# Prologue of a four-layer kernel: low parts of five units on VectorE, distance table first, first pair's rows requested at the fourth unit, maxima stored by ScalarE's queue

## The chip, the cores and the metric

The kernel runs on one core of one Trainium2 chip. The metric is the device time in microseconds (us) of one execution, given as the median of several; lower is better. Engines are named as the profile names them: PE (TensorE matmul), PEld (its weight loads), DVE (VectorE), ACT (ScalarE), POOL (GpSimd), SP (SyncE, which here only issues DMAs). "SPq" is SP's own instruction stream; "DMA queue" is what it hands transfers to.

## The reference, cut to what matters

Four post-norm layers follow one another: softmax attention with a distance decay, an FP4-quantised gated FFN, linear attention, and a mixture of experts. The change touches only what stands ahead of the first one.

```python
q = (x @ Wq.T + bq).reshape(B, T, H, hd)        # B=2, T=2048, D=256, H=16, hd=16
k = (x @ Wk.T + bk).reshape(B, T, H, hd)
v = (x @ Wv.T + bv).reshape(B, T, H, hd)
scores = jnp.einsum('bqhd,bkhd->bhqk', q, k) * scale
scores = scores * jnp.exp(-alpha * lag)          # lag = |i - j|
attn = softmax(scores); out = attn @ v
```

## The kernel before

The kernel is a row of stages, each a block in which the five engines run their own instruction streams; a stage begins when every engine has left the one before. The first stage, `stage_prologue`, makes q, k and v; the second, `stage_attention`, goes through 16 pairs of heads (`Pair`).

**Units.** The prologue works through `GROUPS` = 16 units. Unit u is batch u // 8, half `jt` of the 256 columns of q and k (u // 4 % 2), and a chunk of 512 positions (u % 4). For a unit PE computes a q tile and a k tile (`project`, four matmuls; it is called for unit u + 1 in steps 4 and 5 of unit u), ACT copies them to `full` (L531, L534), and POOL makes one or two versions of q scaled by the table `grow` (L597). So a unit has three or four variants: KEY, LEFT and/or RIGHT, RAW. Each variant is split into three bf16 parts that add up to the f32 value: ACT writes the high part (L545), DVE subtracts it (`split`, L610), ACT writes the middle part (`middle`, L512), and POOL subtracts that and writes the low part (`low`, L559). POOL does `low(u - 1)` in the pass for unit u. `full` has three buffers (`FULLS`), so ACT's evacuation of unit u waits for the low parts of unit u - 3.

**Stores and loads.** When a unit's low parts are done, SP stores its parts to DRAM with four DMAs of 384 KB (L415, into `scr`); units with `jt` = 1 also have v, which SP stores with one DMA of 1 MB (L422, into `vscr`). Units 0 to 3 hold every position of the first eight heads, so they hold all rows of the first pair, `Pair(0, 0)`. SP requests those rows with `load_p1`: 12 DMAs (L312) into `p1`, for q and for k, for two heads each, in three runs of 3, 2 and 1 times 16 rows of 4 KB (`RUNS`). This is written after the stores of unit 4 (`if u == QB`). `load_p2` (18 DMAs) and the second pair's `load_p1` come behind units 7 and 9.

**Tiles.** With the first pair's rows PE and DVE find the largest score of each row ahead of the attention: 128 tiles, each one matmul of 512 columns (L474) and one multiply-and-max on DVE with the distance table `toep` (L626), through two PSUM banks (`PBANKS`). They are spread evenly over the steps of the units from `WITH_TILES` on (`tiles_behind`). After unit 15 come 26 tiles of the second pair and one transposition of the maxima (`SKEWED`), after which `turn_maxima` writes `mt` and `mparts`; SP stores these and loads them again (`store_maxima` and `load_maxima`, 4 and 8 DMAs).

**Small pieces.** POOL clears two borders of `part` (L574, L575), makes `toep` in its pass for unit 1 (L581), and clears 24 rows of `p2[0]` in its pass for unit 3 (L589). A table of decay factors goes from DVE (`cev`, L658, written at the start of DVE's pass for unit 2) to DRAM and back into `p2[0]` by SP (L402, six DMAs, and L405, two); SP does this ahead of all stores of units.

DVE stores a v tile into one of two buffers and, from the third unit with v on, first waits until the DMA of the v before last has landed (`vout`).

Of the kernel before, what the change touches and what calls it, by code (L numbers as in the profile page):

```python
# [6 lines left out]
ALU = mybir.AluOpType  # L7
# [37 lines left out]
    "p_": "loaded dist expd ident cdist cexp csplit ctr cev prep wload xload0 xload1 qk_ps v_ps vout qk_ev "  # L45
          "v_ev scaled hi rest mid low out0 out1 vset",
    "a_": "setup waug p1load0 p1load1 p2load0 p2load1 vload0 vload1 mload0 mload1 mbc ring_full ring_free "
# [48 lines left out]
def up_to(n):  # L96

    return n + 1
# [168 lines left out]
FULLS = 3  # L267
WITH_TILES = 5
STEPS = 8
# [89 lines left out]
def stage_prologue(nc, g, a, p1, p2, vp, mx):  # L359

    with ExitStack() as ctx:
# [24 lines left out]
        def chunk_of(u):  # L386

            b, jt, chunk = place(u)
            return b * QB + chunk if jt else None

        with nc.Block() as block:
            @block.sync
            def _(sp):
# [5 lines left out]
                sp.dma_start(bv[:], a["bv"].partition_broadcast(P)).then_inc(s["wload"], 16)  # L399
                sp.wait_ge(s["cev"], up_to(1))  # L400
                for r, e in enumerate(K_PARTS):
                    sp.dma_start(g["w6"][r].rearrange("q (t p) -> (q t) p", p=P), wt[:, e, :]).then_inc(s["loaded"], 16)  # L402
                sp.wait_ge(s["loaded"], up_to(48 + 16 * 6))
                for hh in range(2):
                    sp.dma_start(p2[0][ROWS:ROWS + AUG, hh, KEY, :],  # L405
                                 g["w6"].rearrange("r q t -> (r q) t")).then_inc(sa["waug"], 16)
# [100 lines left out]
            def _(act):  # L507
# [11 lines left out]
                for u in range(GROUPS):  # L519
# [7 lines left out]
                    if u >= FULLS:  # L527

                        act.wait_ge(s["low"], up_to(parts_upto(u - FULLS + 1)))
                    act.wait_ge(s["qk_ps"], up_to(2 * u + 1))  # L530
# [11 lines left out]
                    for i, var in enumerate(parts_of(u)):  # L542
                        if var in (LEFT, RIGHT):
                            act.wait_ge(s["scaled"], up_to(scaled_upto(u) + i))
                        act.activation(part[:, chunk, var, 0, :], full[:, u % FULLS, var, :], ACT.Copy).then_inc(s["hi"], 1)  # L545
                middle(GROUPS - 1)

            @block.gpsimd
            def _(pool):
# [6 lines left out]
                def low(u):  # L556
                    for i, var in enumerate(parts_of(u)):
# [15 lines left out]
                                   base=0, pattern=[[-1, P]], channel_multiplier=1).then_inc(s["ident"], 1)  # L573
                pool.memset(part[:, 0, LEFT, :, :], 0.0).then_inc(s["ident"], 1)  # L574
                pool.memset(part[:, QB - 1, RIGHT, :, :], 0.0).then_inc(s["ident"], 1)  # L575
                pool.sem_inc(sa["exp"], EXP0)
                pool.sem_inc(sa["value"], PV0)
                pool.sem_inc(sa["evac"], EV0)
                for u in range(GROUPS):
                    if u == 1:  # L580
                        pool.iota(toep[:], [[-1, TOEP]], base=OFF, channel_multiplier=1,  # L581
                                  allow_small_or_imprecise_dtypes=True).then_inc(s["dist"], 1)
                    if u == 0:
                        load_x(2)
                        load_x(3)
                    if u == 3:
                        pool.wait_ge(s["scaled"], up_to(scaled_upto(u)))
                        pool.wait_ge(s["low"], up_to(parts_upto(u - 1)))
                        pool.memset(p2[0][ROWS:ROWS + AUG, :, LEFT:RIGHT + 1, :], 0.0).then_inc(sa["setup"], 1)  # L589
                        pool.wait_ge(sa["setup"], up_to(1))  # L590
                    if QB < u <= 2 * QB:
# [12 lines left out]
            def _(dve):  # L604
# [16 lines left out]
                def tile(slot, j, n):  # L621
# [6 lines left out]
                                             mp[:, j, hh * TB + qt, kc:kc + 1]).then_inc(sa["ring_free"], 1)  # L628

                dve.wait_ge(s["loaded"], up_to(48))  # L630
                dve.tensor_scalar(nalpha[:], alpha[:], -1.0, None, ALU.mult).then_inc(s["prep"], 1)
# [23 lines left out]
                for u in range(GROUPS):  # L655
                    if u == 2:
                        dve.wait_ge(s["ctr"], up_to(1))
                        dve.tensor_copy(wt[:], ps_t).then_inc(s["cev"], 1)  # L658
                        dve.memset(vsb[:], 0.0).then_inc(s["vset"], 1)
                        dve.wait_ge(s["vset"], up_to(1))  # L660
                        dve.memset(vsb[:, :, :, :, :, HD:HD + 1], 1.0).then_inc(s["vset"], 1)
                        dve.wait_ge(s["vset"], up_to(2))
# [11 lines left out]
                for i, n in enumerate(SKEWED):  # L674
# [4 lines left out]
                    else:  # L679
                        tile(slot, 1, n)  # L680
                dve.wait_ge(s["ident"], up_to(4))

# [1902 lines left out]
```

## Time and profile before

| what | value |
|---|---|
| median of 3 runs | 3417.16 us (3413.48, 3422.5, 3417.16) |
| the profiled execution, its own time | 3417.1 us |
| its span, first to last instruction | 3415.3 us |
| mean granted TensorE clock | 0.95 |
| first instruction of the attention stage | 282.49 us into the span |

The prologue is thus 8% of the span. A timeline row reads: start, length, engine, line, operation, written tile <- read tile, count, and in brackets how long the engine had been idle before it and what ended that.

### The profile page before, as it was taken

What the parts mean: (1) busy time and instruction counts of PE and PEld (TensorE: products, weight loads), DVE (VectorE), ACT (ScalarE), POOL (GpSimd) and SP (SyncE); (2) the same over time, 40 slices, a digit from 0 to 9 for tenths busy, and PEclk for the clock granted to TensorE, in tenths of its full rate; (3) what the DMA queues carried; (4) which work ended last, traced back from release to release, by engine and by line L of the source; (5) the groups of instructions that cost most, each with busy time, mean ns of one, the idle gap of its engine ahead of it and who ended that gap; (6) DMA issues with size and microseconds to landing.
All of it is one profiled execution on the core that took longest, in us unless ns stands there. A gap on an engine that the chain in (4) does not pass through costs nothing. (4 is left out here: it accounts for less than half of the span.)

```text
span 3415.3 us, 66017 instructions
## 1 busy us (share of the span) xinstructions
PE 3071.1 (90%) x22948; PEld 1734.7 (51%) x22949; DVE 2440.1 (71%) x6509; ACT 1802.2 (53%) x2255; POOL 1422.7 (42%) x741
## 2 busy tenths in 40 slices
PE   3678999999999999999985998989999987999996
PEld 1232333333333333333323565556666666999995
DVE  4679999999999999999747888844555554333334
ACT  4235888888888888888873333322222222111112
POOL 6346787878878787787801000000000111111110
PEclk7788999999999999999997999989899988999998
DMA  5575434332344443333204110030000005555555
GB/s 154 144 192 138 90 84 83 79 78 76 67 91 92 93 89 82 83 79 78 57 13 78 25 38 5 1 99 14 14 14 14 23 18 191 183 182 177 182 184 182
DMA packets 201698, 304.65 MB, mean 89 GB/s; under 512 B 86192, under 2 KB 150544, under 8 KB 199248
## 3 DMA queue, kind: packets, MB, share of 16 engines
q1 hardware_dynamic: 192640, 277.89, 31.6%
q0 software_dynamic: 7632, 22.16, 1.8%
q8 instruction: 159, 2.61, 0.3%
q14 instruction: 115, 0.94, 0.1%
q10 hardware_dynamic: 1152, 1.05, 0.1%
HBM read 238.91 MB, written 62.13 MB: 88 GB/s over the span
## 5 line engine op out<-in xcount | busy, mean ns | idle before, releaser
L870 DVE CUSTOM_DVE_ANT_0 ps_r<-ps_r,toep 128x512 f32<-128x512 f32 x1894 | 1252.3, 716 | 71.8 <-PE ps_r L799 31.6
L969 ACT ACTIVATE prob<-ps_s,csc 128x1024 f32<-128x1024 f32 x768 | 829.9, 1118 | 151.4 <-PE ps_s L823 129.6
L927 POOL TENSOR_TENSOR tb<-tb,toep 128x1024 f32<-128x1024 f32 x240 | 568.1, 2367 | 264.0 <-ACT tb L959 229.4
L799 PE MATMUL ps_r<-p 96*128 96x512 bf16 x1894 | 646.3, 382 | 10.1 <-DVE mp L870 4.1
L823 PE MATMUL ps_s<-p 120*128 120x512 bf16 (+1 forms) x2048 | 609.3, 380 | 27.1 <-ACT tb L959 16.4
L930 POOL TENSOR_TENSOR tb<-tb,mb 128x1024 f32<-128x1024 f32 x240 | 567.8, 2366 | 18.8
L839 PE MATMUL ps_o<-prob,vp 128*32 128x256 f32 x8192 | 548.2, 385 | 1.2 <-ACT prob L966 0.9
L799 PEld LDWEIGHTS ps_r<-p 96*128 96x128 bf16 x1894 | 181.4, 96 | 406.2 <-DVE mp L870 258.0
L1695 POOL DMA_INDIRECT slots_scratch<-l_xh,l_place x64 | 62.5, 976 | 710.3 <-DVE l_xh L2020 693.3
L839 PEld LDWEIGHTS ps_o<-prob,vp 128*32 128x32 f32 x8192 | 213.7, 109 | 269.6 <-issue 177.9
L823 PEld LDWEIGHTS ps_s<-p 120*128 120x128 bf16 (+1 forms) x2048 | 189.6, 98 | 237.2 <-ACT tb L959 46.6
L2335 ACT ACTIVATE e_aT<-e_u 128x1024 f32<-128x1024 f32 x71 | 75.0, 1057 | 421.4 <-DVE e_u L2406 421.4
L966 ACT ACTIVATE prob<-tb 128x1024 f32<-128x1024 f32 x256 | 272.3, 1064 | 2.9 <-POOL tb L930 2.8
L2281 PEld LDWEIGHTS ps_eu<-e_hT,moe_w 128*128 128x128 f32 x2272 | 266.3, 193 | 7.7 <-DVE e_hT L2397 4.1
L2281 PE MATMUL ps_eu<-e_hT,moe_w 128*128 128x128 f32 x2272 | 266.9, 276 | 3.5 <-DVE e_hT L2397 3.5
L870 DVE DVE_READ_ACCUMULATOR2_ANT mp<- 128x1 f32 x1894 | 266.2, 141 | 0.0
L959 ACT ACTIVATE tb<-ps_s 128x1024 f32<-128x1024 f32 x240 | 247.0, 1029 | 32.7 <-PE ps_s L823 31.3
L2374 POOL DMA_INDIRECT ytok_scratch<-e_y,e_name x71 | 69.2, 975 | 463.0 <-DVE e_y L2452 463.0
L2299 PE MATMUL ps_ed<-moe_w,e_aT 128*128 x1136 | 257.0, 379 | 0.8 <-DVE e_y L2452 0.8
L2406 DVE TENSOR_TENSOR e_u<-ps_eu,moe_cols 128x1024 f32<-128x1024 f32 x71 | 86.9, 1224 | 210.1 <-PE ps_eu L2281 210.1
L2299 PEld LDWEIGHTS ps_ed<-moe_w,e_aT 128*128 128x128 f32 x1136 | 210.3, 190 | 26.9 <-issue 1.2
L1280 PE MATMUL ps_du<-wgu,d_xs 128*128 128x512 f32 (+1 forms) x384 | 164.6, 580 | 4.2 <-DVE d_h L1559 2.6
(324 smaller groups left out, 3580.4 us busy)
## 6 DMA issues: line engine op xcount, KB each, us to landing
moe_w<-in_W_dram SPq DMA_DIRECT2D x79, 1024.0 KB, 5.3
p<-scr_scratch SPq DMA_DIRECT2D x288, 192.0 KB
mb<-mrow_scratch SPq DMA_DIRECT2D x16, 2048.0 KB, 7.4
scr_scratch<-part SPq DMA_DIRECT2D x64, 384.0 KB, 6.7
p<-scr_scratch SPq DMA_DIRECT2D x96, 128.0 KB
moe_pt<-slots_scratch SPq DMA_DIRECT2D x72, 132.0 KB, 2.1
vscr_scratch<-vsb SPq DMA_DIRECT2D x8, 1024.0 KB, 8.8
vp<-vscr_scratch SPq DMA_DIRECT2D x16, 512.0 KB, 22.2
```

Source lines behind the costliest of these rows:

```text
L799: pe.matmul(ps_r[:, bank, :], buf[:, hh, 0, qt * P:(qt + 1) * P], buf[:, hh, 1, kc * CH:(kc + 1) * CH], start=True, stop=True)\
L823: mm = pe.matmul(ps_s[:, n % 2, hh, :], buf[0:rows, hh, KEY, kb * P:(kb + 1) * P], buf[0:rows, hh, var, qb * CH:(qb + 1) * CH], start=True ...
L839: mm = pe.matmul(out.rearrange("p (j c) -> p j c", c=P), vp[whose.par][:, kb, hh, :], prob[:, m % RING, hh, :].rearrange("p (j f c) -> p f ...
L870: dve.tensor_tensor_reduce(ps_r[:, bank, :], ps_r[:, bank, :], toep[:, col:col + CH], 1.0, -3.0e38, ALU.mult, ALU.max, mp[:, whose.par, hh ...
L927: pool.tensor_tensor(tb[:, k % DIAGS], tb[:, k % DIAGS], toep[:, col:col + CH].unsqueeze(1) .broadcast_to([P, 2, CH]), ALU.mult).then_inc( ...
L930: pool.tensor_tensor(tb[:, k % DIAGS], tb[:, k % DIAGS], mb[:, this.par, :, qb * CH:(qb + 1) * CH], ALU.add).then_inc(s["less"], 1)
L959: act.activation(tb[:, k % DIAGS], ps_s[:, (mine - 1) % 2], ACT.Copy).then_inc(s["copied"], 1)
L966: act.activation(prob[:, n % RING], tb[:, k % DIAGS], ACT.Exp).then_inc(s["exp"], 1)
L969: act.activation(prob[:, n % RING], ps_s[:, mine % 2], ACT.Exp, scale=csc[:, qb * TB + kb:qb * TB + kb + 1]).then_inc(s["exp"], 1)
L1280: mm = pe.matmul(ps_u[:, lo:hi], xs[:, c % 2, kc, t * P:(t + 1) * P], wgu[:, kc, lo:hi], start=(kc == 0), stop=(kc == KC - 1), skip_group_ ...
L2281: mm = pe.matmul(ps_u[:, tile.par, f, :], w1[:, tile.par, kc, f * P:(f + 1) * P], hT[:, kc, :], start=(kc == 0), stop=(kc == KC - 1), skip ...
L2299: mm = pe.matmul(ps_d[:, 0:D], aT[:, this.par, f, :], w["w2"][:, bass.ds(e, 1), f, :].rearrange("p a n -> p (a n)"), start=(f == 0), stop= ...
```

## The change

Five things are done at once in `stage_prologue`; no arithmetic of the result changes.

1. The low parts of units 0 to 4 (`LOW_FIRST` = 5) are made on DVE, in a function `low` of its own that counts on a semaphore `lowv`; POOL makes those of units 5 to 15. Whoever waits for low parts asks `low_done`.
2. `toep` is made by POOL before its loop over units. The two borders of `part` and the 24 rows of `p2[0]` are cleared by DVE.
3. SP stores units 0 and 1 first, then sends the decay table out and back, then goes on with unit 2. It requests the first pair's rows right behind unit 3, once the stores of units 0 to 3 have landed.
4. `WITH_TILES` is 6: PE waits for the first pair's rows at unit 6, not at unit 5, and the 128 tiles are spread over ten units.
5. The maxima are stored and loaded by ACT's queue, after ACT's last middle part.

```diff
-WITH_TILES = 5
+WITH_TILES = 6
+LOW_FIRST = 5
...
+        def low_done(eng, u):
+            if u < LOW_FIRST:
+                eng.wait_ge(s["lowv"], up_to(parts_upto(u + 1)))
+            else:
+                eng.wait_ge(s["low"], up_to(parts_upto(u + 1) - parts_upto(LOW_FIRST)))
...
             def _(sp):
...
-                sp.wait_ge(s["cev"], up_to(1))
-                for r, e in enumerate(K_PARTS):
-                    sp.dma_start(g["w6"][r].rearrange("q (t p) -> (q t) p", p=P), wt[:, e, :]).then_inc(s["loaded"], 16)
...
                 for u in range(GROUPS):
-                    sp.wait_ge(s["low"], up_to(parts_upto(u + 1)))
+                    low_done(sp, u)
...
+                    if u == 1:
+                        sp.wait_ge(s["cev"], up_to(1))
+                        for r, e in enumerate(K_PARTS):
+                            sp.dma_start(g["w6"][r].rearrange("q (t p) -> (q t) p", p=P), wt[:, e, :]).then_inc(s["loaded"], 16)
...
-                    if u == QB:
-                        sp.wait_ge(s["out1"], up_to(64 * 2))
+                    if u == QB - 1:
+                        for n in range(2):
+                            sp.wait_ge(s[f"out{n}"], up_to(64 * 2))
                         load_p1(sp, Pair(0, 0))
...
-                sp.wait_ge(sa["setup"], up_to(1))
-                sp.wait_ge(sa["ring_free"], up_to(TILES + TURN + 1))
-                store_maxima(sp, g, sa, mt, mparts)
-                sp.wait_ge(sa["mstore"], up_to(64))
-                load_maxima(sp, g, sa, p2[0], "mload0")
...
             def _(act):
...
+                act.wait_ge(sa["setup"], up_to(1))
+                act.wait_ge(sa["ring_free"], up_to(TILES + TURN + 1))
+                store_maxima(act, g, sa, mt, mparts)
+                act.wait_ge(sa["mstore"], up_to(64))
+                load_maxima(act, g, sa, p2[0], "mload0")
...
             def _(pool):
...
-                    if u:
+                    if u > LOW_FIRST:
                         low(u - 1)
...
             def _(dve):
...
+                    if u == 3:
+                        dve.memset(p2[0][ROWS:ROWS + AUG, :, LEFT:RIGHT + 1, :], 0.0).then_inc(sa["setup"], 1)
...
+                    if 1 <= u <= LOW_FIRST:
+                        low(u - 1)
```

**SP, from the first store on.** In the kernel before, the order of DMA issues on SP is this (`w_scratch` and `p_0<-w_scratch` are the decay table, `scr_scratch<-part` the stores of units, four each, `p_0<-scr_scratch` the first pair's rows):

```order
L402 DMA w_scratch<-wt 64x128 x6
L405 DMA p_0<-w_scratch 24x2048 x2
L415 DMA scr_scratch<-part 32x12x512 x20
L422 DMA vscr_scratch<-vsb 128x8x256
L312 DMA p_0<-scr_scratch 48x1x2048 x2
L312 DMA p_0<-scr_scratch 32x1x2048 x2
```

In the changed kernel (its lines are numbered anew):

```order
L415 DMA scr_scratch<-part 32x12x512 x8
L427 DMA w_scratch<-wt 64x128 x6
L430 DMA p_0<-w_scratch 24x2048 x2
L415 DMA scr_scratch<-part 32x12x512 x8
L313 DMA p_0<-scr_scratch 48x1x2048 x2
L313 DMA p_0<-scr_scratch 32x1x2048 x2
```

Two units' stores moved ahead of the table, and one unit's stores and one store of v moved behind the request.

**DVE, its passes for units 0 to 4.** Before, DVE has only its subtractions and the start of the v buffer there:

```order
L610 TENSOR_TENSOR full<-full,part 128x512 x7
L658 COPY wt<-ps_pr 64x384
L659 MEMSET vsb 128x4096
L661 MEMSET vsb 128x128
L610 TENSOR_TENSOR full<-full,part 128x512 x10
```

In the changed kernel the low parts (L634) stand between them, and the clearing of `p_0`'s rows (L673), which is written there as 2 x 2048 elements:

```order
L611 TENSOR_TENSOR full<-full,part 128x512 x3
L634 TENSOR_TENSOR part<-full,part 128x512 x3
L611 TENSOR_TENSOR full<-full,part 128x512 x4
L667 COPY wt<-ps_pr 64x384
L668 MEMSET vsb 128x4096
L670 MEMSET vsb 128x128
L634 TENSOR_TENSOR part<-full,part 128x512 x4
L611 TENSOR_TENSOR full<-full,part 128x512 x4
L673 MEMSET p_0 24x2x2048
L634 TENSOR_TENSOR part<-full,part 128x512 x4
L611 TENSOR_TENSOR full<-full,part 128x512 x3
L634 TENSOR_TENSOR part<-full,part 128x512 x3
```

**POOL, the same stretch.** Before, POOL's order there, its low parts being L559 and the clearing of the same rows L589 (written as 2 x 4096 elements):

```order
L559 TENSOR_TENSOR part<-full,part 128x512 x3
L597 TENSOR_TENSOR full<-full,grow 128x512 x2
L559 TENSOR_TENSOR part<-full,part 128x512 x4
L589 MEMSET p_0 24x2x4096
L597 TENSOR_TENSOR full<-full,grow 128x512
L559 TENSOR_TENSOR part<-full,part 128x512 x4
```

In the changed kernel seven scalings (L598) follow one another with nothing between them:

```order
L583 IOTA toep 128x3968
L562 DMA xc<-in_xT_dram 128x2x512 x2
L598 TENSOR_TENSOR full<-full,grow 128x512 x7
L562 DMA xc<-in_xT_dram 128x2x512
```

What left POOL here is the seventeen low parts of units 0 to 4 and the clearing; the table `toep` moved ahead of its first scaling.

## Rows read from the trace of the kernel before

**Rows 1.** The page, its head.

```profile
span 3415.3 us, 66017 instructions
```

**Rows 2.** Waits of 0 to 282 us: who for whom, total, times, longest.

```profile
PE ps_v L464 <- DMA p<-scr_scratch: 58.3, 1, 58.3
...
DVE vsb L618 <- DMA vscr_scratch<-vsb: 7.0, 1, 7.0
```

**Rows 3.** Timeline of PE around the first pair's rows.

```profile
42.73 3.70 PE L454 MATMUL ps_qk<-xc,w_qkv 128*128 128x512 f32 x8 [1.64 <-ACT full L534]
104.74 2.04 PE L464 MATMUL ps_v<-w_qkv,xc 128*128 128x256 f32 x4 [58.30 <-DMA p<-scr_scratch]
...
111.50 1.88 PE L454 MATMUL ps_qk<-xc,w_qkv 128*128 128x512 f32 x4
...
124.52 1.88 PE L454 MATMUL ps_qk<-xc,w_qkv 128*128 128x512 f32 x4
```

**Rows 4.** Timeline of SP's issues, from several windows of 30 to 105 us.

```profile
33.02 3.72 SPq L402 DMA_DIRECT2D w_scratch<-wt  x6
...
38.85 11.87 SPq L415 DMA_DIRECT2D scr_scratch<-part  x8
...
65.69 3.27 SPq L415 DMA_DIRECT2D scr_scratch<-part  x2
...
75.38 15.75 SPq L312 DMA_DIRECT2D p<-scr_scratch  x12
```

**Rows 5.** Five-us windows: PE, PEld, DVE, ACT, POOL busy; clock, DMA share, GB/s.

```profile
85.00:90.00 5.00, 0.00 (x0) 0.00 (x0) 0.00 (x0) 0.00 (x0) 0.00 (x0) 0.50 0.19 73
...
95.00:100.00 5.00, 0.00 (x0) 0.00 (x0) 0.00 (x0) 0.00 (x0) 0.00 (x0) 0.50 0.13 52
```

**Rows 6.** Timeline of POOL: the clearing, and unit 3's low parts.

```profile
41.38 6.92 POOL L589 MEMSET p<- 24x8192 bf16 x1
...
56.62 4.27 POOL L559 TENSOR_TENSOR part<-full,part 128x512 bf16<-128x512 f32 x3
```

**Rows 7.** Timeline of DVE: the start of the v buffer.

```profile
33.80 3.47 DVE L659 MEMSET vsb<- 128x4096 f32 x1 [0.80 <-issue]
```

**Rows 8.** Timeline of ACT: middle parts of unit 2.

```profile
42.56 2.19 ACT L512 ACTIVATE part<-full 128x512 bf16<-128x512 f32 x4
```

**Rows 9.** DVE's subtractions, 20 to 62 us: ns min/median/max.

```profile
L610 DVE TENSOR_TENSOR full<-full,part x18: 678/1096/6816, 23.0 to 61.2; 128x512 f32<-128x512 f32 x18
```

**Rows 10.** Stores of units (line L415), 30 to 68 us, and the smallest load.

```profile
DMA to landing us min/median/max: 3.5/6.3/7.4
...
alpha<-in_alpha_dram SPq DMA_DIRECT2D x1, 0.5 KB, 2.3
```

**Rows 11.** Costliest groups of 0 to 330 us: the tiles on DVE.

```profile
L626 DVE CUSTOM_DVE_ANT_0 ps_pr<-ps_pr,toep 128x512 f32<-128x512 f32 x154 | 103.9, 704 | 62.3 <-PE ps_pr L474 61.7
```

**Rows 12.** Timeline of DVE and PE to the end of the prologue.

```profile
242.30 0.42 DVE L618 TENSOR_TENSOR vsb<-ps_v,bv 128x256 f32<-128x256 f32 x1 [6.95 <-DMA vscr_scratch<-vsb]
...
260.01 0.28 DVE L673 TENSOR_REDUCE nm<-mp 128x32 f32<-128x128 f32 x1
...
263.42 0.28 DVE L339 TENSOR_TENSOR mparts<-ps_pr,mparts 32x128 bf16<-32x128 f32 x1
...
280.28 0.14 DVE L626 DVE_READ_ACCUMULATOR2_ANT mp<- 128x1 f32 x1
282.53 1.44 PE L799 MATMUL ps_r<-p 96*128 96x512 bf16 x3 [2.90 <-PEq L391]
```

**Rows 13.** Timeline of SP's issues from unit 7's stores on.

```profile
146.96 4.44 SPq L415 DMA_DIRECT2D scr_scratch<-part  x4
...
171.50 12.64 SPq L415 DMA_DIRECT2D scr_scratch<-part  x1
...
266.89 5.56 SPq L346 DMA_DIRECT2D m_scratch<-mparts  x3
...
277.83 3.74 SPq L356 DMA_DIRECT2D p<-m_scratch  x5
```

More of the change, by code:

```diff
@@ L45 @@
     "p_": "loaded dist expd ident cdist cexp csplit ctr cev prep wload xload0 xload1 qk_ps v_ps vout qk_ev "
-          "v_ev scaled hi rest mid low out0 out1 vset",
+          "v_ev scaled hi rest mid low lowv out0 out1 vset",
     "a_": "setup waug p1load0 p1load1 p2load0 p2load1 vload0 vload1 mload0 mload1 mbc ring_full ring_free "
@@ L399, in _ @@
                 sp.dma_start(bv[:], a["bv"].partition_broadcast(P)).then_inc(s["wload"], 16)
-                sp.wait_ge(s["cev"], up_to(1))
-                for r, e in enumerate(K_PARTS):
-                    sp.dma_start(g["w6"][r].rearrange("q (t p) -> (q t) p", p=P), wt[:, e, :]).then_inc(s["loaded"], 16)
[L403 to L406, printed above, removed]
                 for u in range(GROUPS):
                     b, jt, chunk = place(u)
-                    sp.wait_ge(s["low"], up_to(parts_upto(u + 1)))
+                    low_done(sp, u)
                     sp.wait_ge(s[f"out{u % 2}"], up_to(64 * (u // 2)))
@@ L423, in _ @@
                                      vsb[:, c % 2].rearrange("p a t h d -> p a (t h d)")).then_inc(s["vout"], 16)
-                    if u == QB:
-                        sp.wait_ge(s["out1"], up_to(64 * 2))
+                    if u == 1:
+                        sp.wait_ge(s["cev"], up_to(1))
+                        for r, e in enumerate(K_PARTS):
+                            sp.dma_start(g["w6"][r].rearrange("q (t p) -> (q t) p", p=P), wt[:, e, :]).then_inc(s["loaded"], 16)
+                        sp.wait_ge(s["loaded"], up_to(48 + 16 * 6))
+                        for hh in range(2):
+                            sp.dma_start(p2[0][ROWS:ROWS + AUG, hh, KEY, :],
+                                         g["w6"].rearrange("r q t -> (r q) t")).then_inc(sa["waug"], 16)
+                    if u == QB - 1:
+                        for n in range(2):
+                            sp.wait_ge(s[f"out{n}"], up_to(64 * 2))
                         load_p1(sp, Pair(0, 0))
@@ L527, in _ @@
                     if u >= FULLS:
-                        act.wait_ge(s["low"], up_to(parts_upto(u - FULLS + 1)))
+                        low_done(act, u - FULLS)
                     act.wait_ge(s["qk_ps"], up_to(2 * u + 1))
@@ L573, in _ @@
                                    base=0, pattern=[[-1, P]], channel_multiplier=1).then_inc(s["ident"], 1)
-                pool.memset(part[:, 0, LEFT, :, :], 0.0).then_inc(s["ident"], 1)
-                pool.memset(part[:, QB - 1, RIGHT, :, :], 0.0).then_inc(s["ident"], 1)
+                pool.iota(toep[:], [[-1, TOEP]], base=OFF, channel_multiplier=1,
+                          allow_small_or_imprecise_dtypes=True).then_inc(s["dist"], 1)
                 pool.sem_inc(sa["exp"], EXP0)
@@ L579, in _ @@
                 for u in range(GROUPS):
-                    if u == 1:
-                        pool.iota(toep[:], [[-1, TOEP]], base=OFF, channel_multiplier=1,
-                                  allow_small_or_imprecise_dtypes=True).then_inc(s["dist"], 1)
                     if u == 0:
@@ L585, in _ @@
                         load_x(3)
[L586 to L590, printed above, removed]
                     if QB < u <= 2 * QB:
@@ L628, in tile, with low @@
                                              mp[:, j, hh * TB + qt, kc:kc + 1]).then_inc(sa["ring_free"], 1)
+                def low(u):
+                    for i, var in enumerate(parts_of(u)):
+                        dve.wait_ge(s["mid"], up_to(parts_upto(u) + i + 1))
+                        dve.tensor_tensor(part[:, u % QB, var, 2, :], full[:, u % FULLS, var, :], part[:, u % QB, var, 1, :],
+                                          ALU.subtract).then_inc(s["lowv"], 1)
+                dve.memset(part[:, 0, LEFT, :, :], 0.0).then_inc(s["vset"], 1)
+                dve.memset(part[:, QB - 1, RIGHT, :, :], 0.0).then_inc(s["vset"], 1)
                 dve.wait_ge(s["loaded"], up_to(48))
@@ L659, in _ @@
                         dve.memset(vsb[:], 0.0).then_inc(s["vset"], 1)
-                        dve.wait_ge(s["vset"], up_to(1))
+                        dve.wait_ge(s["vset"], up_to(3))
                         dve.memset(vsb[:, :, :, :, :, HD:HD + 1], 1.0).then_inc(s["vset"], 1)
-                        dve.wait_ge(s["vset"], up_to(2))
+                        dve.wait_ge(s["vset"], up_to(4))
+                    if u == 3:
+                        dve.memset(p2[0][ROWS:ROWS + AUG, :, LEFT:RIGHT + 1, :], 0.0).then_inc(sa["setup"], 1)
                     if u == WITH_TILES:
                         dve.wait_ge(s["expd"], up_to(3))
+                    if 1 <= u <= LOW_FIRST:
+                        low(u - 1)
                     for step in range(STEPS):
@@ L680, in _ @@
                         tile(slot, 1, n)
-                dve.wait_ge(s["ident"], up_to(4))
+                dve.wait_ge(s["ident"], up_to(2))
 def stage_attention(nc, g, a, p1, p2, vp0, mx):
```

## The prediction, made before the changed kernel ran

> **What bounds the kernel now.** The span is 3415.3 us [rows 1] and its own run took 3417.1 us, 0.06 us under the median of 3417.16 shown, so a sum made on the span can be taken from the median as it is. The stages run one after the other and the change edits only the first, so I ask what ends it. I read the waits first. Up to 282 us there is one wait of 58.3 us, of PE for the first pair's rows, and one of 7.0 us, of DVE for a store of v [rows 2]. Then the timeline of PE: it ends its matmuls for unit 5 at 42.73 + 3.70 = 46.4 and starts again at 104.74 [rows 3]. Every engine stands still at the end of this hole, and all that follows hangs on its end, which I call T: 104.74.
>
> Then SP's issues, for what makes T. The decay table goes first, at 33.02, and the first store of a unit starts at 38.85; two units take 11.87 us to issue; the last issue for unit 3 starts at 65.69 (the first of two in that row); then come unit 4 and a store of v, and the request goes out at 75.38 [rows 4]. From there to T are 29.3 us. In the windows, 85 to 90 us has a DMA share of 0.19 at 73 GB/s, and 95 to 100 us 0.13 at 52 GB/s [rows 5]: 3 and 2 engines of 16, some 24 to 25 GB/s each. So the end of the load is a few engines with too many rows, and bandwidth is not what it lacks.
>
> Behind T, DVE and PE go through units together, about 13.0 us each (111.50 to 124.52, [rows 3]). DVE has its last tile of 128 done at 260.01 and its last instruction at 280.28; the attention starts at 282.53 [rows 12]. SP leaves the stage with its last issue at 277.83 + 3.74 = 281.57 [rows 13], so today the maxima on SP end the stage, 1.15 us behind DVE's 280.42 (280.28 + 0.14), and the change of stage takes another 0.96.
>
> **The load itself.** All of it is 12 DMAs. Of four of them each carries 48 rows of 4 KB, of four 32 rows, of four 16 rows. If a DMA is spread over as many engines as its run has groups (3, 2, 16), the busiest engine carries 4 x (16 + 16 + 1) = 132 rows, 0.54 MB, and at 24 to 25 GB/s needs 21.6 to 22.5 us; the shares of 3 and 2 engines [rows 5] fit. I take 22, and for the start the 2.3 us in which the smallest load lands [rows 10]: 24.3 us on an idle queue. The other 5 us of today's 29.3 are then backlog: unit 4's stores and the store of v go ahead of the rows. They stand behind the request now. If instead backlog had made all of it, an idle queue would need 8 us (1.6 MB, where two units' stores, 3.1 MB, take 16.7 from first issue to landing, below) and T would come 16 us sooner still; the stretch of 85 to 100 us at 2 to 3 engines without any other traffic speak against that. The Trainium skill has a rule for this in "DMA: Bandwidth & Descriptors", section on why a DMA increments its semaphore by 16: the number of engines is the largest up to 16 that divides the slowest dimension of both sides, from the lowest-numbered on. By it the 3- and 2-group DMAs share the same first engines whatever is queued, 132 rows; by an even spread over 16 it would be 24 rows and some 4 us. The trace's 0.19 and 0.13 agree with the rule.
>
> **When the request goes out now.** I replay the first 70 us. ACT, PE and DVE's first splits are unchanged to 25 us.
> - Low parts of unit 0 on DVE: ACT's middle parts end at about 27.3, DVE follows by 28.5. One such two-input operation costs DVE 0.68 us at best and 1.10 in the middle of today's rows, where POOL works beside it [rows 9]. POOL now has only its scalings, so I take 0.6 to 0.7 (starts overlap a little), and 1.2 while POOL scales. Its cost where both run at once is the bound: 17 low parts at 1.1 are 19 us, at 0.6 are 10. Unit 0's stores go out at 28.5, not 38.85.
> - DVE's split of unit 1 to 31, the table's copy, the start of the v buffer. That row says 3.47 but has 0.80 before it with nothing to wait for [rows 7]: 4.27 us for 4096 elements. Low parts of unit 1: 36.1 to 38.5. Split of unit 2 to 40.9.
> - The clearing of `p2[0]`'s rows: 6.92 us on POOL for 8192 elements [rows 6]. On DVE the order writes it as 2 x 2048 = 4096 elements, as many as the v buffer has: 4.27 us, to 45.2. If it cost by its bytes' bf16 elements, 8.5. The Trainium skill ("VectorE: DVE Perf Modes", zero memsets as uint32) says one cycle per element whatever the type, and half the elements when written as uint32; by it 4.3, by POOL's row 6.9. I take 4.3.
> - Unit 2's middle parts are there at 44.75 [rows 8], so its low parts end at 47.9. Unit 3: POOL's scaling is no longer behind the clearing, split to 49.9, middle parts to 51, low parts 51.6, against 60.9 today [rows 6].
> - SP: unit 1 38.5 to 43.1; the six DMAs of the table 3.7 us [rows 4] to 46.8, whose landing waits behind unit 1's data, about 48.3; two more to 49.2. So SP, not the low parts, sets unit 2's start: 49.2. Eight issues without a gap take 11.87 us, the last starts 1.5 before that end and lands 6.3 later [rows 4, 10]: 49.2 + 16.7 = 65.9. The x for unit 9, asked for at 57 and not behind T as now, costs 1: 66.9.
>
> T is then 66.9 + 24.3 = 91.2, **13.5 us sooner**. If the memset costs 8.5 it is 11; if DVE runs all its pairs at 1.2, 10; if the table lands without delay, 15.
>
> **What follows T.** Unit 5's values, splits and projection now lie in the hole. It took 13.0 us, of which 11.6 tiles (128 over 11 units) at 0.70 [rows 11] were 8.1; those tiles still have to be done. Gain 13.0 - 8.1 = 4.9. The wait of 7.0 us is for a store that SP issued late: it landed 95.3 us after unit 7's stores went out (146.96 to 242.30, [rows 12, 13]), with SP busy all the while. Unit 7's stores start at T + 42.2 now, at T + 30.6 afterwards (a unit less, 1.3 us more tiles), so the store lands at T + 125.9, and DVE gets there at about T + 124.4: 1.5 of the 7.0 stay, gain 5.5. At the end ACT stores the maxima. They are ready 16.7 us before DVE's end (263.70 against 280.42, [rows 12]), and SP's chain took 266.89 to 281.57 = 14.7 [rows 13], so it fits with 2 us to spare; DVE's end is what counts, gain 1.15. The stores of unit 15 end on SP 14 us before DVE. Together **11.5 us**, between 5 (the wait of 7 stays) and 13.
>
> A rule speaks against the last part. The Trainium skill, "DMA: Bandwidth & Descriptors", "Issuing engines are not separate DMA queues": the queues of SP and ACT share the 16 engines, so a second one saves issue time alone. By it the maxima travel no faster on ACT. No run here shows it yet; my 1.15 us is only the wait for SP's place in the row.
>
> Sum: 13.5 + 11.5 = 25.0; the span goes to 3390 and the median from 3417.2 to **3392 us**. Costed at nothing: the borders of `part` on DVE (it waits to 10.2 us for its first input), `toep` before the loop on POOL (POOL then idles to 20 us), DVE's low parts of unit 4 (in the hole).
>
> **Rivals.**
> - *The forecast*: T 10 to 15 sooner, 8 to 13 behind it; 3387 to 3399. Chance 0.64.
> - *The stores give it back.* The table's eight DMAs stand between units 1 and 2, and DVE's passes grow by low parts at 1.1 us and a memset by bytes. Then unit 3 lands at 71 as now, T gains only the 5 us of backlog, and the wait for v grows back to 7: 5 + 6 = 11, 3406. For it: SP's issues of 1.5 us are paced by transfers. Against: today the first store waits to 38.85 with nothing in the queue. Chance 0.16.
> - *Nothing to measure.* A further backlog: the stores of units 4 and 5 and their v all follow T, since SP sits behind a load that holds it as it did for 12.64 us [rows 13]; DVE then waits for the v buffer in unit 6 by over 10 us, and again later. 15 lost of 25, or more: 3407 to 3417. Chance 0.06.
> - *More*: the low parts of unit 2 decide, the table costs nothing, T at 84, no v wait: 3383. Chance 0.09.
> - *Slower*: ACT's chain of maxima. It begins at T + 148 and its issues and loads share engines with unit 15's stores. If one issue is held 12.64 us as SP's was [rows 13] and so are two more, the chain ends 38 us late; with 2 us to spare and 25 gained it decides from 27 us on, and at 38 gives 3428. Against: what held SP then was a load of rows on few engines, and none is in flight at that time. Chance 0.05.
>
> **Range and chances.** From 3382 to 3407 it leaves out the slower case, the most of the third, and some of the ends, 0.15. A change under 0.3% (10 us, about what three runs that spread over 9 us can tell) is the third case and a part of the second: 0.09. Faster by more: 0.86, slower: 0.05.
>
> **What would show it.** Right: SP's first store near 28 us, the request for the first pair's rows near 67, PE's wait for it ending near 91 with 24 to 25 us from request to landing, the attention's first matmul near 258. DVE's memset of `p_0` near 4.3 us. Wrong: a request behind 72 (SP's or DVE's part), a load of well over or under 24 us (the engines' part), a DVE wait for `vscr` in units 6 or 7, or SP or ACT ending the stage behind DVE.

## The result and the profile after

| | before | after |
|---|---|---|
| median of 20 runs, us | 3422.23 (3412.15 to 3448.53) | 3401.30 (3391.79 to 3428.38) |
| profiled execution, its own time, us | 3417.1 | 3414.64 |
| first instruction of the attention stage | 282.5 | 261.4 |
| prologue / attention / dense | 282.5 / 1509.0 / 445.5 | 261.4 / 1510.7 / 446.3 |
| linear attention with router / experts | 600.7 / 577.7 | 616.6 / 577.9 |

The ratio is 0.9941, 95% interval 0.9918 to 0.9964: 20 us faster (12 to 28 by the interval). The forecast was 25.0 (3417.2 to 3392). The median after lies 9 us above the forecast's 3392: 4 us of that are gain that did not come, and 5 us are the median before, which is 3422 over 20 runs where the forecast started from 3417 over 3. The table cuts each span at the first instruction of every stage. The prologue gave 21.1 us, which agrees with the medians; the two profiled executions stand only 2.5 us apart, because a stage that the change does not touch took 16 us more in the second. Two windows from the middle of that stage, of the kernel after and of the experiment below in which it took 596.6 us (span, then PE, PEld, DVE, ACT, POOL busy; granted clock as a share of 2.4 GHz, DMA share, GB/s), show what went with it. After:

```profile
2420.00:2520.00 100.00, 93.65 (x811) 64.73 (x814) 48.83 (x151) 23.94 (x43) 15.48 (x16) 0.88 0.06 23
2520.00:2620.00 100.00, 92.28 (x863) 62.32 (x858) 50.49 (x137) 25.71 (x48) 7.75 (x8) 0.81 0.04 12
```

Experiment e5:

```profile
2420.00:2520.00 100.00, 92.19 (x820) 62.05 (x816) 53.83 (x157) 28.40 (x51) 15.54 (x16) 0.98 0.06 23
2520.00:2620.00 100.00, 92.05 (x1046) 65.25 (x1045) 56.42 (x171) 28.18 (x53) 7.77 (x8) 0.91 0.04 12
```

PE is as busy, at a granted clock 0.10 lower. Over all profiles of this study the stage took either 593 to 601 us or 616 to 620, with any prologue in front; what lowers the clock no run here shows. So from here on each kernel is judged by its prologue: when the request for the first pair's rows goes out, when PE's wait for them ends (T), when the 128 tiles are folded (DVE's TENSOR_REDUCE), and the first matmul of the attention. The same kernel profiled twice (e8, e11) differed by 2.3, 2.7, 2.5 and 2.5 us in these four, so a difference under 2 to 3 us says nothing here.

The timeline of SP in the kernel after, which answers to [rows 4]:

```profile
29.55 14.27 SPq L415 DMA_DIRECT2D scr_scratch<-part  x8
43.86 6.38 SPq L427 DMA_DIRECT2D w_scratch<-wt  x6
53.53 0.72 SPq L430 DMA_DIRECT2D p<-w_scratch  x2
54.35 12.41 SPq L415 DMA_DIRECT2D scr_scratch<-part  x8
71.83 11.95 SPq L313 DMA_DIRECT2D p<-scr_scratch  x12
83.89 9.93 SPq L415 DMA_DIRECT2D scr_scratch<-part  x4
93.92 2.06 SPq L422 DMA_DIRECT2D vscr_scratch<-vsb  x1
```

Unit 0's stores go out at 29.55, 1 us behind the forecast (28.5). Then the decay table takes until 54.35: 6.38 us of issue, which took 3.72 in [rows 4], and 3.3 us in which SP waits for the last of the six to land. That wait is not for unit 1's data, which had landed at 48.57. POOL asked for 512 KB of x at 49.13; they landed at 53.31, and the last of the six at 53.51. In e1 below POOL asks for x only at 54.10, and there the last of the six lands 1.8 us after its issue. Unit 2's stores start at 54.35, the request at 71.83 where 66.9 was forecast. PE, around the wait that [rows 3] show:

```profile
62.47 3.60 PE L458 MATMUL ps_qk<-xc,w_qkv 128*128 128x512 f32 x8
96.95 2.05 PE L468 MATMUL ps_v<-w_qkv,xc 128*128 128x256 f32 x4 [30.89 <-issue]
...
104.78 1.88 PE L458 MATMUL ps_qk<-xc,w_qkv 128*128 128x512 f32 x4
...
261.42 1.44 PE L812 MATMUL ps_r<-p 96*128 96x512 bf16 x3 [1.76 <-PEq L399]
```

T is 96.95, 7.8 us sooner than before. The 30.89 us bear the word "issue" because the profile found no releaser; PE waits there on the semaphore of the load, and in e9 below the same wait bears the load's name. DVE between 29 and 55 us, and at the places that [rows 12] show:

```profile
42.66 3.47 DVE L673 MEMSET p<- 24x4096 uint32 x1 [0.91 <-issue]
46.16 3.57 DVE L634 TENSOR_TENSOR part<-full,part 128x512 bf16<-128x512 f32 x4
49.66 1.88 DVE L611 TENSOR_TENSOR full<-full,part 128x512 f32<-128x512 f32 x3
51.46 1.89 DVE L634 TENSOR_TENSOR part<-full,part 128x512 bf16<-128x512 f32 x3
...
221.03 0.42 DVE L619 TENSOR_TENSOR vsb<-ps_v,bv 128x256 f32<-128x256 f32 x1 [2.71 <-DMA vscr_scratch<-vsb]
...
240.04 0.29 DVE L686 TENSOR_REDUCE nm<-mp 128x32 f32<-128x128 f32 x1
```

Unit 2's low parts end at 49.73, 4.6 us before SP is free for them. The waits of 0 to 262 us give for v, as total, times and longest (7.0 in [rows 2]):

```profile
DVE vsb L619 <- DMA vscr_scratch<-vsb: 3.5, 2, 2.7
```

From T to the fold are 143.1 us (155.3 before), from there to the attention 21.4 (22.5 before).

One reading of the kernel before has to be put right, since the argument hangs on it. The first store does not start at 38.85 because low parts are late. Those of unit 0 are done on POOL at 31.58; SP still has the table ahead of all stores, and is through with it at 38.74. For units 2 and 3 it is the other way round: there SP waits for POOL, until 54.98 and 60.89 ([rows 6] have the second).

```profile
27.28 4.30 POOL L559 TENSOR_TENSOR part<-full,part 128x512 bf16<-128x512 f32 x3
...
49.60 5.38 POOL L559 TENSOR_TENSOR part<-full,part 128x512 bf16<-128x512 f32 x4
```

```profile
37.99 0.75 SPq L405 DMA_DIRECT2D p<-w_scratch  x2
...
55.02 4.46 SPq L415 DMA_DIRECT2D scr_scratch<-part  x4
```

### The profile page after: what moved, and what is told of

It reads as the page before. It is cut to its first block and busy times, and to the rows that moved or that the text cites. A ratio compares the mean times of both kernels' runs of the same rounds, so it can differ in the third digit from the quotient of the medians.

```text
span 3412.9 us, 66017 instructions
## 1 busy us (share of the span) xinstructions
PE 3093.8 (91%) x22948; PEld 1750.5 (51%) x22949; DVE 2444.9 (72%) x6529; ACT 1802.6 (53%) x2255; POOL 1390.8 (41%) x721
## 5 line engine op out<-in xcount | busy, mean ns | idle before, releaser
L2060 DVE TENSOR_TENSOR l_sm<-ps_ls,l_tri 128x256 f32<-128x256 f32 x256 | 96.0, 419 | 101.7 <-PE ps_ls L1810 92.9
```

The lines of the kernel that those rows point to most:

```text
L2060: dve.tensor_tensor(sm[:, k % 2, i:i + HG // 2], ps_s[:, k % 2, i:i + HG // 2], tri[:].unsqueeze(1).broadcast_to([P, HG // 2, P]), ALU.mul ...
```

## The experiments

The theory after the result: the request came 5 us late for the table between units 1 and 2, the load is held by three busy engines, and most of the rest is the tiles' later start. Rivals: that low parts on DVE or ACT's queue carry the gain, and that the load is slowed by other traffic.

**e1: low parts back on POOL.**

```diff
-LOW_FIRST = 5
+LOW_FIRST = 0
```

> The changed kernel with LOW_FIRST = 0: all low parts on POOL again, everything else as changed. Numbers are of the trace, in us into the span; the changed kernel has: first store issued 29.6, unit 1's 39.4, unit 2's 54.4, request of the first pair's rows 71.8, PE's wait for them ends 96.95, attention's first matmul 261.4. Theory (SP's order with the table between units 1 and 2 sets the request, the low parts hardly do): low parts of unit 0 end near 32, of unit 1 near 41.5, unit 2's stores go out near 56.5, PE's wait ends at 98 to 100, attention at 262 to 265. Rival (the low parts on DVE are what made the request early): the request at 77 or later, PE's wait ends at 102 or later, attention at 267 or later.

SP's timeline:

```profile
31.80 14.18 SPq L415 DMA_DIRECT2D scr_scratch<-part  x8
46.03 6.36 SPq L427 DMA_DIRECT2D w_scratch<-wt  x6
53.63 0.72 SPq L430 DMA_DIRECT2D p<-w_scratch  x2
54.45 12.31 SPq L415 DMA_DIRECT2D scr_scratch<-part  x8
72.81 11.76 SPq L313 DMA_DIRECT2D p<-scr_scratch  x12
```

Units 0 and 1 start 2.3 us later, but unit 2 only 0.1 us, since the table stands ahead of it either way. T 97.78, attention at 260.97, 0.5 us sooner than with the low parts on DVE; own time 3400.63. The theory's 98 and 262 are missed by a little, towards still less effect. The move of seventeen low parts shows no gain in this order. Nor does POOL need help for the first store: it has unit 0's low parts at 31.78, as before the change (31.58), and the store now follows at 31.80, because the table no longer stands ahead of it.

**e2: the request behind unit 4 again** (all else as after).

```diff
-                    if u == QB - 1:
+                    if u == QB:
                         for n in range(2):
```

> The changed kernel with the request of the first pair's rows put back behind unit 4's stores and the store of v. Theory (backlog ahead of the rows cost 5 us, and the place in the row the rest): the request at about 75.5, 29 us from request to the end of PE's wait as before the change, so 104 to 105, which is 7 to 8 us later than in the changed kernel (96.95); attention's first matmul 7 us later, 268 to 269. Rival (the load takes 25 us wherever it stands, because its length is set by engines alone): PE's wait ends at 100 to 101. Second rival (what stands behind the request costs as much as what stands ahead): the attention moves by under 3 us, since DVE's waits for the v buffer shrink.

Request 75.89, T 103.81, attention 267.80 (6.4 us later), own time 3405.15. The request is 4.1 us later, the load another 2.8 us longer (27.9 against 25.1), since unit 4's stores and a v stand ahead of it: both parts count, as the theory had it (104 to 105, 268 to 269).

**e3: the table behind the request.** The block of `if u == 1` moves under `if u == QB`, behind the request.

> The changed kernel with the decay table's eight DMAs behind the request (after unit 4's stores) instead of between units 1 and 2. Theory (the table is what held unit 2's stores from 49.7, when its low parts were done, to 54.4): unit 2's stores go out at 49.7 to 50.2, the request at 67 to 67.5, PE's wait ends at 92 to 92.7, attention 4 to 5 us earlier than 261.4: 256.5 to 257.5. Rival (stores are paced by the transfers, so the table only filled time in which the queue was full): the request at 70 to 72, attention at 260 to 261.5.

```profile
28.48 32.70 SPq L415 DMA_DIRECT2D scr_scratch<-part  x16
66.37 12.22 SPq L313 DMA_DIRECT2D p<-scr_scratch  x12
78.71 10.18 SPq L415 DMA_DIRECT2D scr_scratch<-part  x4
88.99 1.62 SPq L422 DMA_DIRECT2D vscr_scratch<-vsb  x1
90.65 9.91 SPq L432 DMA_DIRECT2D w_scratch<-wt  x6
```

The request goes out at 66.37, 5.5 us sooner. PE:

```profile
91.53 2.05 PE L468 MATMUL ps_v<-w_qkv,xc 128*128 128x256 f32 x4 [27.14 <-issue]
```

T is 5.4 us sooner at the same load (25.2), the attention starts at 255.73, 5.7 sooner; own time 3388.67. These are close to the forecast's own 66.9 and 91.2. In the forecast unit 2's low parts were done 1.3 us before SP was through with the table, so without the table its sum gives 65.6 and 89.9: the rest of the first term holds to 1 or 2 us, and the table is the step that was off.

**e4: tiles from unit 5 on** (`WITH_TILES = 5`).

> The changed kernel with WITH_TILES = 5: PE waits for the first pair's rows at unit 5 again, and its values, unit 6's projection and so on follow the wait. Theory (unit 5's work without tiles, 4.9 us, lay in the hole): PE's wait ends at 96 to 97 as before or 1 us earlier, attention at 265 to 267.5, 4 to 6 us later than 261.4. Rival (SP's row of stores and loads sets the end of the prologue whatever PE and DVE do): attention within 1.5 us of 261.4, with a longer wait of DVE for a store of v.

T 95.12, but the fold at 250.06 and the attention at 270.80, 9.4 us later; own time 3406.35. T to fold is 154.9 us, as before the change (155.3), against 143.1: the later start of the tiles carries 11.8 of the 13.3 us gained behind T, 2.4 of them through DVE's wait for v, which is 5.88 here against 3.5. The theory had taken the forecast's 4.9 us and expected 4 to 6, so it missed by 4; where they come from is worked out below.

**e5: the maxima back on SP.** The five lines of the diff's point 5 return to SP's block, ahead of its last waits.

> The changed kernel with the maxima stored and loaded by SP again, behind its last stores. In the changed kernel the maxima are ready at 243.7 and SP issues its last store of v at 243.6 to 245.0, DVE's part ends near 260.3. Theory (the move to ACT is worth 0 to 1 us, since SP is free at the moment the maxima are ready): SP's chain of 14.7 us runs from 245 to 259.7, attention's first matmul at 260.4 to 262 (changed kernel: 261.4). Rival (the queue is the point: on SP the maxima stand behind stores that are held): SP's chain ends at 264 or later, attention at 265 or later.

```profile
242.89 1.95 SPq L422 DMA_DIRECT2D vscr_scratch<-vsb  x1
244.94 5.08 SPq L347 DMA_DIRECT2D m_scratch<-mparts  x3
250.07 0.42 SPq L348 DMA_DIRECT2D mrow_scratch<-mt  x1
252.41 6.49 SPq L357 DMA_DIRECT2D p<-m_scratch  x8
```

The same chain on ACT:

```profile
243.81 4.68 ACTq L347 DMA_DIRECT2D m_scratch<-mparts  x3
248.52 1.75 ACTq L348 DMA_DIRECT2D mrow_scratch<-mt  x1
254.12 6.50 ACTq L357 DMA_DIRECT2D p<-m_scratch  x8
```

From fold to attention are 20.9 us on SP (238.89 to 259.83) and 21.4 on ACT; own time 3396.31. SP loses 2 us behind the store of v and has it back in shorter landings and issues: its chain takes 14.0 us, ACT's 16.8. The queue shows no gain. This is what the Trainium skill says in "DMA: Bandwidth & Descriptors", "Issuing engines are not separate DMA queues": a second issuing engine saves issue time alone.

**e6: the first pair's rows in DMAs of 16 rows.** 24 DMAs instead of 12, the same bytes.

```diff
+            def load_first(sp):
+                for into, var in enumerate((RAW, KEY)):
+                    for r in range(len(Q_PARTS)):
+                        e = (K_PARTS if var == KEY else Q_PARTS)[r]
+                        for hh in range(2):
+                            src = g["scr"][0:1, var, e:e + 1, hh * HD:(hh + 1) * HD].rearrange("a e d t -> (a e) d t")
+                            sp.dma_start(p1[0][HD * r:HD * (r + 1), hh, into, :], src).then_inc(s["wload"], 16)
```

> The changed kernel with the first pair's rows requested by 24 DMAs of 16 rows, where 12 of 48, 32 and 16 rows stood; same bytes. Theory (a DMA of 48 rows runs on 3 engines and one of 32 on 2, the same ones each time, so the busiest carries 132 rows; in DMAs of 16 rows it carries 24): from request to the end of PE's wait 12 to 17 us, set by SP's issues of 0.4 to 0.7 us, where it was 25.1; PE's wait ends at 84 to 89. The attention gains less, since unit 4's store of v then lands too late for DVE in unit 6: a wait of 5 to 10 us there, attention at 253 to 258 (was 261.4). Rival (the load's length comes from latency or from the DRAM side, not from engines): 22 us or more from request to the end of the wait, attention at 260 to 262.

SP's request, PE behind it, and a window of five us between:

```profile
71.40 11.25 SPq L406 DMA_DIRECT2D p<-scr_scratch  x24
```

```profile
85.53 2.04 PE L476 MATMUL ps_v<-w_qkv,xc 128*128 128x256 f32 x4 [19.68 <-issue]
```

```profile
75.00:80.00 5.00, 0.00 (x0) 0.00 (x0) 0.00 (x0) 0.00 (x0) 0.00 (x0) 0.50 0.54 139
```

The same window of the kernel after:

```profile
75.00:80.00 5.00, 0.00 (x0) 0.00 (x0) 0.00 (x0) 0.00 (x0) 0.00 (x0) 0.50 0.30 78
```

The load takes 14.1 us instead of 25.1, at a DMA share of 0.54 instead of 0.30. And 11.25 us of issue and 2.9 us in which one such DMA lands (median in the view of the DMAs) are 14.15: that is the whole load, so by this sum SP's issuing, 0.47 us for each, now bounds it. The attention starts at 247.56, 13.9 us sooner, 2.5 more than T: of the wait for v 1.8 us are left, from 3.5. The theory had feared 5 to 10 us of that wait and an attention at 253 to 258. Own time 3376.31. By the rule of the Trainium skill that the prediction named ("DMA: Bandwidth & Descriptors", section on why a DMA increments its semaphore by 16), a DMA of three groups runs on three engines and one of 16 rows on 16. The traces agree with the first (0.19 of 16 engines, three, in [rows 5]); for the second they show 0.54 in the window above, nearly nine, so many more than three at once but not the number itself.

**e7 and e8: what the experiments point to.** In both the table's six DMAs go behind unit 4 and its two behind unit 8, the clearing of `p2[0]` is back on POOL in unit 3, and v is stored ahead of the unit's parts. In e7 the first pair's rows alone are loaded 16 rows a DMA, in e8 those of all sixteen pairs.

```diff
     def load(sp, dst, var, into, j, sem):
-        for r, n in RUNS:
-            first = 0 if var == KEY else Q_PARTS[r]
+        for r, n in ((r, 1) for r in range(6)):
+            first = (K_PARTS if var == KEY else Q_PARTS)[r]
```

> Four edits on the changed kernel: the table's six DMAs behind unit 4's stores and its last two behind unit 8's; the clearing of p2's rows back on POOL in its pass for unit 3; the first pair's rows in 24 DMAs of 16 rows; each unit's store of v ahead of its parts. From theory: unit 2's stores go out at 45 (DVE has 4.4 us less ahead of its low parts), the request at 62.5 to 64, PE's wait ends at 75 to 80, the wait for a store of v in unit 6 stays under 3 us, attention's first matmul at 240 to 245. Rival (behind the load the stores set the pace of the prologue, so that what the start gains is given back): attention at 250 or later, with DVE's waits for stores of v of more than 8 us in sum.

> As the kernel before it in this call, but every load of rows (load_p1 and the key part of load_p2, in the prologue and in the attention) goes in DMAs of 16 rows: 24 instead of 12 for load_p1 and 24 instead of 18 for load_p2. Theory: in the prologue SP is no longer held behind loads (one issue of 9.5 us and others of 3 to 5 in the changed kernel), so DVE's late wait for v goes and the attention begins 1 to 3 us sooner than with the first pair alone; the attention itself, 1510.7 us in the changed kernel, stays within 2 us, since its loads are hidden. Rival: more DMAs cost SP 0.45 us each, 270 us over the attention, and where SP is late the attention is 5 us longer or more.

e7: request 64.36, T 78.48, fold 219.98, attention 242.0, as expected, but that unit 2's low parts were done at 46.5 rather than 45 and the request went out 0.4 us late; own time 3393.08, of which the stage with the router took 616. e8: request 65.58, T 79.81, fold 220.24, attention 240.97, no wait for v at all; own time 3374.17. The attention stage takes 1510.2 us in e8 and 1510.7 after, so the sixteen pairs gain nothing by shorter loads, which are hidden there.

**e9: the kernel before, with the request alone moved.**

```diff
-                    if u == QB:
-                        sp.wait_ge(s["out1"], up_to(64 * 2))
+                    if u == QB - 1:
+                        for n in range(2):
+                            sp.wait_ge(s[f"out{n}"], up_to(64 * 2))
                         load_p1(sp, Pair(0, 0))
```

> The kernel before with one edit of the change alone: the request of the first pair's rows right behind unit 3's stores. Low parts, table, WITH_TILES and maxima are as before. Before: request 75.4, PE's wait ends 104.7, attention's first matmul 282.5. Theory (backlog is worth 4 to 5 us, and the row's place 2): unit 3's last issue ends near 67.5 and lands near 72, so the request is at 71.5 to 72.5 and PE's wait ends at 96.5 to 98, which is 7 to 8 us sooner; attention at 274 to 276.5. Rival (the forecast's view that the earlier low parts and the moved table were most of the 7.8 us): PE's wait ends at 101 or later.

```profile
33.17 3.72 SPq L402 DMA_DIRECT2D w_scratch<-wt  x6
38.13 0.75 SPq L405 DMA_DIRECT2D p<-w_scratch  x2
39.00 28.48 SPq L415 DMA_DIRECT2D scr_scratch<-part  x16
71.65 11.62 SPq L312 DMA_DIRECT2D p<-scr_scratch  x12
```

PE, at T:

```profile
96.37 2.04 PE L465 MATMUL ps_v<-w_qkv,xc 128*128 128x256 f32 x4 [49.92 <-DMA p<-scr_scratch]
```

Request 71.65, T 96.37, attention 273.91. Own time 3430.27, with 620 us in the stage with the router. With nothing else changed T comes 8.4 us sooner; the whole change brought 7.8. The first store starts 9.4 us later than in the kernel after (39.00 and 29.55) and the request goes out at the same time: from first store to request SP needs 32.65 us here and 42.28 there. Of the 9.4 us the table's new place (part 3) brought 7, since unit 0's low parts were done at 31.7 here too, and low parts on DVE the other 2.3 (e1). They do not reach the request. Here unit 2's stores wait for POOL until 55.0, in the kernel after for the table until 54.35: the change took one brake away and put another in the same place.

**e10: e8 with the low parts on POOL and the clearing on DVE.**

> The best version so far (table late and split, all rows in DMAs of 16, store of v first) with the clearing on DVE again and all low parts on POOL. With low parts on DVE it had unit 2's stores at 47.6, the request at 65.6, PE's wait to 79.8, attention at 240.9. Theory (with the table gone from between units 1 and 2 the low parts show again, and POOL is 2 us later for units 0 and 1 and 3 for unit 3): unit 2's stores near 48.5, unit 3's near 54.5, the request at 67 to 69, PE's wait ends at 81 to 83.5, attention at 242 to 245. Rival (low parts on DVE are worth nothing in any order, because stores are paced by their transfers): within 1 us of all these times.

Request 66.09, T 80.19, attention 241.57, own time 3377.31: 0.5, 0.4 and 0.6 us behind e8, 3 behind e11. This is what the rival said, not the theory (T 81 to 83.5, attention 242 to 245). With the table out of the way, too, the low parts on DVE are worth 0 to 3 us, no more than two profiles of one kernel differ.

**e11: e8 again, timed.**

> The version with all loads of rows in DMAs of 16 rows again, now timed. Its prologue was 20.5 us shorter than the changed kernel's (240.9 against 261.4) and 41.6 shorter than before. Theory: the median is 38 to 46 us under that of the kernel before, ratio 0.986 to 0.989, and attention takes 1509 to 1511 us. Rival (something behind the prologue gives part back that one profile did not show): ratio over 0.991.

3380.75 us median of 6 runs, before 3426.71 of 11, ratio 0.9876 (0.9847 to 0.9904): by the ratio 42 us under before, where the change has 20. Prologue 238.5 us, 44.0 less than before; attention 1510.0, experts 578.2, as in the other runs.

## Why the prediction was right, and where its sums were off

The time lies in the range, with 4 us less gained than forecast: 21.1 of 25.0 in the prologue. The sum came this near partly by luck. Its terms were off by -5.7 us (T), +3.8 (tiles) and -2.0 (wait for v), and the first two, from unrelated causes, set each other off. T came 7.8 us sooner, outside the 10 to 15 that the forecast's own case allowed, and 3401.3 us is outside its 3387 to 3399; only the wider range holds. Of the signs of being wrong, one came close (a request behind 72; it was 71.83) and two came in small: a wait of DVE for a store of v in unit 7, 0.8 us, and ACT ending the stage behind DVE, by 0.2 us.

- **The hole's end decides: right.** T came 7.8 us sooner and what follows it took 13.3 less, 21.1 in all. e2, e3 and e6 move T by 6.9, 5.4 and 11.4 us, and the attention by 6.4, 5.7 and 13.9.
- **The first term, 13.5 us, was 7.8, and the step that failed is the table's.** "The six DMAs of the table 3.7 us to 46.8, whose landing waits behind unit 1's data, about 48.3; two more to 49.2" put 6.1 us on it; it took 10.5. The 3.7 us were read from a row in which nothing stood ahead of these six in the queue; behind eight stores the issue took 6.4, and the landing 3.3 more, beside the x that POOL had asked for. That is 4.4 of the 4.9 us by which the request was late; the table also began 0.8 later than forecast (43.86 for 43.1), and from unit 2's start to the request were 17.5 us where 17.7 was forecast, 1 of it for x. e3 is the test: without the table the request goes out at 66.4. Behind this lies a reading that was wrong: "today the first store waits to 38.85 with nothing in the queue". It waited for the table, not for low parts. So the start of the stores at 28.5, which the sum puts down to low parts on DVE, came mostly from moving the table, and the same table then held unit 2. e9 shows what is left: the request's new place alone gives 8.4 us of T, and low parts, clearing and table together, for which the forecast had some 5 of its 13.5, gave nothing. That a rival named the same table ("the stores give it back") with the mechanism of low parts at 1.1 us did not make it right: they took 0.62 to 0.96 each, as means of a unit.
- **The load, 24.3 us, was 25.1: right**, and its cause, too. 132 rows on the busiest engine are an estimate of 22 us and 2.3 of start; in pieces of 16 rows, same bytes, the load takes 14.1. The 5 us of backlog were 4.6 (29.3 before, 24.7 in e9).
- **The memset, 4.3 us: right.** 0.91 + 3.47 = 4.38 for 4096 elements of uint32. Low parts of unit 3 ended at 53.35 where 51.6 was forecast, and SP came later still, as forecast.
- **Behind T 11.5 us was 13.3, with errors on both sides.** The path from T to the fold shrank by 12.2 us (155.3 to 143.1), 3.5 of it by a shorter wait for v, so the tiles' later start gave 8.7, where 4.9 stood. One window over each path, before and after (span, then PE, PEld, DVE, ACT, POOL busy; clock, DMA share, GB/s), says why:

```profile
104.74:260.01 155.27, 116.39 (x321) 52.89 (x321) 121.98 (x323) 52.59 (x94) 68.96 (x57) 0.84 0.74 183
```

```profile
96.95:240.04 143.09, 109.49 (x297) 47.91 (x297) 117.20 (x315) 46.95 (x84) 60.84 (x50) 0.85 0.80 208
```

At a like granted clock DVE's busy time fell from 121.98 to 117.20, by 4.8, which is the forecast's 4.9. But its idle time fell as well, from 33.3 to 25.9, by 7.4, of which the wait for v is 3.5. The other 3.9 are idle time of DVE in the units, which shrank as the moved tiles came in; the forecast charged the tiles their full time, 8.1 us, and they cost about 4.3. Over the same units, from the projection for unit 7 to that for unit 15, a unit takes 13.66 us before and 14.00 after, 0.34 more and not 0.81. The wait for v went to 3.5, not 1.5: gain 3.5, not 5.5. The tail gave 1.1, where 1.15 stood, but not for the reason given: e9, with SP as before, has 20.7 us from fold to attention, e5 20.9, after 21.4. That part is the difference between executions, and that it met the forecast is luck.
- **What the parts are worth**, in us of the attention's start. Three steps lead from the kernel before to the kernel after and add up to the 21.1. The request behind unit 3 alone: 8.6 (282.5 to 273.9, e9; taken back from the kernel after it is 6.4, e2). Then low parts, clearing and `toep`, the table and ACT's queue all together: 3.1 (273.9 to 270.8, from e9 to e4). Then the tiles from unit 6 on: 9.4 (270.8 to 261.4, from e4 to after). The 3.1 is hardly more than one kernel differs from itself. Within it low parts on DVE show -0.5 (e1) and ACT's queue -1.6 (e5), both losses and both within that difference; how the rest divides no kernel here shows. In e1 and e5 the attention stage itself took 1513.7 and 1514.1 us where the others have 1509.0 to 1510.8, so at the end of that stage the order of the three is turned round; e10 with low parts on POOL, and e9 with low parts on POOL and SP's queue, have 1510, so this is no effect of those two edits, and the differences are too small to rank.
- **The rival with ACT's chain of maxima did not come**: three issues took 4.68 us, the eight loads 6.50, and none was held. But the 2 us to spare were gone: the chain took 16.8 us, not 14.7, and ended at 260.62, DVE at 260.45.

## What to carry to other kernels

Before a step is credited with a delay, ask what the waiting engine had ahead of it in its own order: SP's first store stood behind the table, not behind low parts. A small transfer has another price behind a large one than in an empty queue, and it costs the end nothing only while something else sets the pace: read its cost from a row with the same neighbours, or put it where nobody waits for its queue. A load on whose end everything hangs is worth a look at how many engines it runs on: the same bytes in pieces of 16 rows took 14.1 us instead of 25.1. Work spread over units in which the engine already has gaps costs less than count times duration; work moved to a faster engine gains only if the next step in line is not held by another.

## What the runs showed of the hardware that was not expected

A stage untouched by any edit took 593 to 601 or 616 to 620 us, by execution, at a granted clock of 0.98 and 0.91 (e5, 597 us) or 0.88 and 0.81 (after, 617 us) in the same windows. SP's issue of six small DMAs took 3.72 us with nothing ahead (before, e9), 6.4 behind eight stores (after, e1), and 9.91 behind a pair's load with a unit's stores and a v (e3). The last of the six lands 1.8 us after its issue starts when nothing large is in flight (before, e1), and 3.9 us when 512 KB of x are (after). 24 DMAs of 64 KB are issued in 11.25 us and 12 DMAs of 64 to 192 KB in 11.95: SP pays for the fewer and larger ones as much.
